# Strassen's products for q, k and v, attention per sequence of 64 keys, and the last sum of each rotation on GpSimd

## The reference, cut to what matters

```python
c = x @ W1.T + b1 + 2 * lora(x, adapter of the sequence)     # 1024 -> 1024
q = rope(c @ wq)   # 1024 -> 32 heads of 128
k = rope(c @ wk)   # 1024 ->  8 heads of 128
v = c @ wv         # 1024 ->  8 heads of 128
x1 = x + softmax(mask(q k^T / sqrt(128))) v @ wo             # 4096 -> 1024; the mask is causal within 64 tokens
out = x1 + ffn(cond2(x1))                                    # two more 1024 -> 1024 layers with routed low-rank parts
```

## Time and profile before

| what | value |
|---|---|
| runs, us | 2927.39, 2928.24, 2931.74; median 2928.24 |
| span of the profiled execution | 2929.6 us |
| TensorE busy | 2887.8 us, 99% |
| VectorE busy | 1516.9 us, 52% |
| ScalarE busy | 710.9 us, 24% |
| GpSimd busy | 478.3 us, 16% |
| mean granted TensorE clock | 0.996 |

### The profile page before, as it was taken

One profiled execution on the slowest core, in us unless ns is written; L12 is line 12 of the kernel. 1 busy time (PEld: TensorE's weight loads), 2 busy tenths in 40 slices (PEclk: granted clock), 3 DMA queues, 4 the chain that ended last, 5 costly groups with the idle time before them and its releaser, 6 DMA issues.

```text
span 2929.6 us, 39491 instructions
## 1 busy us (share of the span) xinstructions
PE 2887.8 (99%) x14200; PEld 2407.0 (82%) x14200; DVE 1516.9 (52%) x2443; ACT 710.9 (24%) x1681; POOL 478.3 (16%) x198
## 2 busy tenths in 40 slices
PE   8989999999999999999998999999999999999999
PEld 7867888888888888887876788888888888888887
DVE  2131656465665646565523265646556474656452
ACT  2121223132221313231102131313223131323110
POOL 0020111211111111110302012111111211111030
PEclk9999999999999999999999999999999999999999
DMA  6841111111111111111442111111111111110232
GB/s 214 233 121 37 43 44 36 43 43 42 37 43 43 36 43 43 37 35 55 111 144 60 43 37 49 37 43 36 43 43 36 44 39 45 37 43 29 72 99 68
DMA packets 230725, 174.67 MB, mean 60 GB/s; under 512 B 65146, under 2 KB 198394, under 8 KB 230658
## 3 DMA queue, kind: packets, MB, share of 16 engines
q1 hardware_dynamic: 202850, 151.80, 18.1%
q10 hardware_dynamic: 27808, 22.02, 2.3%
HBM read 151.58 MB, written 22.22 MB: 59 GB/s over the span
## 4 chain that ended last, share of the span: by engine, by line
PE 89%; DVE 5%; issue 2%; ACT 2%; SPq 1%; DMA 0%; ACTq 0%; DVEq 0%
PE prod L529 26%; PE prod L531 25%; PE prod L530 25%; PE turned L726 4%; PE turned L705 2%; PE turned L715 2%; ACT probs L1051 2%; DVE rope_sin L1372 2%; PE turned L523 1%; PE prod L625 1%; PE prod L888 1%; DVE row_max L1385 1%; DVE probs L1382 1%; PE turned L695 0%; PE prod L865 0%
## 5 line engine op out<-in xcount | busy, mean ns | idle before, releaser
L529 PE MATMUL prod<-c_hi,w_hi 128*128 128x512 f32 (+1 forms) x1856 | 737.7, 397 | 3.2 <-DVE c_lo L1445 3.2
L531 PE MATMUL prod<-c_hi,w_lo 128*128 128x512 f32 (+1 forms) x1856 | 724.3, 390 | 0.0
L530 PE MATMUL prod<-c_lo,w_hi 128*128 128x512 f32 (+1 forms) x1856 | 722.7, 389 | 0.0
L1193 POOL TENSOR_TENSOR w_lo<-raw,w_hi 128x1024 fp32r<-128x1024 f32 x160 | 382.1, 2388 | 1844.1 <-ACT w_hi L983 1844.1
L1434 DVE TENSOR_TENSOR x<-prod,x 128x512 f32<-128x512 f32 x512 | 349.4, 690 | 284.0 <-PE prod L531 281.4
L531 PEld LDWEIGHTS prod<-c_hi,w_lo 128*128 128x128 f32 (+1 forms) x1856 | 347.3, 187 | 75.9
L529 PEld LDWEIGHTS prod<-c_hi,w_hi 128*128 128x128 f32 (+1 forms) x1856 | 347.8, 187 | 74.1 <-DVE c_lo L1445 4.0
L530 PEld LDWEIGHTS prod<-c_lo,w_hi 128*128 128x128 f32 (+1 forms) x1856 | 348.1, 188 | 70.5 <-issue 1.0
L529 PE MATMUL prod<-o_hi,w_hi 128*128 128x512 f32 x1024 | 405.0, 395 | 0.0
L531 PE MATMUL prod<-o_hi,w_lo 128*128 128x512 f32 x1024 | 399.4, 390 | 0.0
L530 PE MATMUL prod<-o_lo,w_hi 128*128 128x512 f32 x1024 | 398.8, 389 | 0.0
(11 more groups left out here) (123 smaller groups left out, 2689.4 us busy)
## 6 DMA issues: line engine op xcount, KB each, us to landing
raw<-in_wq SPq DMA_DIRECT2D x64, 512.0 KB, 4.0
raw<-in_wo SPq DMA_DIRECT2D x64, 512.0 KB, 3.8
raw<-t_scratch SPq DMA_DIRECT2D x34, 512.0 KB, 3.5
t_scratch<-x ACTq DMA_DIRECT2D x17, 512.0 KB, 5.0
x_raw<-in_x SPq DMA_DIRECT2D x16, 512.0 KB, 8.8
raw<-in_wk SPq DMA_DIRECT2D x16, 512.0 KB, 3.6
raw<-in_wv SPq DMA_DIRECT2D x16, 512.0 KB, 3.6
raw<-m_scratch SPq DMA_DIRECT2D x16, 512.0 KB, 3.5
```

What stands on the lines that cost most here:

```text
L529: pe.matmul(dst, wh, xh, start=start, stop=False)
L530: pe.matmul(dst, wh, xl, start=False, stop=False)
L531: return pe.matmul(dst, wl, xh, start=False, stop=stop)
L1193: pool.tensor_tensor(WL[j % 2][:], RAW[j % 2][:], WH[j % 2][:].bitcast(F32), ALU.subtract).then_inc(split_d, 1)
```

## The change

**Products.** q, k and v no longer come from `main`. The output of two heads by two token blocks (a quad: k with v, q heads 0 and 1, q heads 2 and 3; three quads for each group) is a 2 x 2 block product with the 1024 inputs cut in two, done as seven products of 12 matmuls each. The seven right sides (`b11`, `b21`, `b22` and four sums) are made once for a half in the W1 stage, in high and low parts. The seven left sides of a quad are blocks or sums of blocks of the weights. GpSimd makes four sums and seven low parts of 512 columns for each quad (the list below), ScalarE the seven high parts (`s_high`). A quad's weights (1 MB) come in one buffer, `RAWP`. `SH`/`SL` have one buffer for each of the seven, so the next quad's high part i waits for product i of this one. ScalarE copies the first product out (`p1_copy`), and VectorE makes the outputs with seven additions of 512 columns; those of a head are added in place in PSUM and rotated from there. In the code PR_1 is product 0, then PR_2, PR_6, PR_7, PR_5, PR_4, PR_3.

**Rotation.** VectorE writes the cosine part to K or Q, and the sine part to a single `RS`; the sum of the two is now a GpSimd instruction (`rotated_sum`), placed between its weight work for the next quad. The next rotation waits for it.

**Attention.** A unit is two heads by 512 tokens, four units for each group. Scores are 16 matmuls of 64 x 64 outputs (`score`), the softmax works on eight blocks of 64 keys, with eight exponentials of 64 columns for each unit, the transposes are four for each unit (`turn_p`), and `pv` is eight matmuls over 64 keys (half the partitions) by 128 columns. v is transposed twice, once shifted by 64 tokens (`turn_v`, 16 transposes for each group). These pieces stand behind products of the next quads (the list `at_`); the last group's stand between the first wo products. The output goes to scratch DRAM by `o_out`: two ScalarE copies to one buffer and a store of 512 KB, each waiting for the store before.

**wo and W1.** The wo products leave the groups and follow all eight: 4 blocks of 1024 rows by 8 tiles by 2 token blocks, `main` each, the same count of matmuls. Their inputs are loaded from scratch (`load_o`, eight loads of 512 KB), and split in 16 pieces by ScalarE (`o_high`) and GpSimd (`o_low`). The W1 stage loads each weight tile twice, once for each token block (`T_WO` is 16 tiles), with the low parts on GpSimd. x goes back to scratch DRAM block by block (`x_back` on GpSimd, `store_xt`) and is read again as `X1`. x comes through four buffers: blocks 4 to 7 are loaded behind the 16 adapter loads in the first half. The second half's blocks 0 to 3 are transposed in the last blocks of the first half, and its 16 adapter loads stand before the load of the last weight tile there. All loops are unrolled in the program. The matmul columns of the first part and of the last stage are the same.

The diff, cut to the waits and orders that the text speaks of:

```diff
+            def store_xt(hf, b):
+                sp.wait_ge(x_sum, hf * TB + b + 1)
...
+            def load_w1(hf, n):
+                if n >= 2:
+                    sp.wait_ge(w_lo, pool_no(hf, n - 2) + 1)
+                load_tile(hf, n, t_d[TW_W + W1_ORDER[n][0]])
...
+            def load_pair(n, hf, g, qd):
+                if g == 0 and qd == 0:
+                    sp.wait_ge(w_lo, pool_no(hf, T_WO - 1) + 1)
+                else:
+                    sp.wait_ge(s_lo, 7 * (n - 1) + 6)
...
+            def load_o(hf, kb):
+                sp.wait_ge(o_stored, 16 * 4 * (hf * NKV + 2 * kb + 2))
+                if kb == 0:
+                    sp.wait_ge(qprod, q_done(pair_no(hf, NKV - 1, QD_23), 3))
...
+                for c in range(KC):
+                    sp.dma_start(chunk_of(o_lows(kb % 2, OWP), c), o_d[kb * KC + c]).then_inc(o_in[c], 16)
...
+                load_b1(hf, 0)
+                for n in range(2, T_WO):
+                    if n - 2 < TB:
+                        store_xt(hf, n - 2)
+                    load_w1(hf, n)
+                    if n == 10:
+                        sp.wait_ge(prod, q_base + QN["c7.0"] + 1)
+                        load_b1(hf, 1)
+                for g in range(NKV):
+                    for qd in range(QUADS):
+                        load_pair(pair_no(hf, g, qd), hf, g, qd)
+                load_wo(hf, 0)
...
-                    for j in range(12):
-                        main(Q_G + j, (j // TT) % 2, j % TT, CH, CL).then_inc(prod, 1)
+                def product(n, i, first):
+                    name, bank = BLOCKS[i], (7 * n + i) % 4
+                    gg, qd = divmod(n, QUADS)
+                    pg, pq = divmod(n - 1, QUADS)
+                    pe.wait_ge(s_lo, 7 * n + LOS[i])
+                    if i == 0 and first:
+                        pe.wait_ge(taken, q_base + Q_WO + 4)
+                    elif i == 0:
+                        pe.wait_ge(quad_in, quad_at(n - 1, A_U3))
+                    elif i in (1, 2) and not first and pq == QD_KV:
+                        pe.wait_ge(quad_in, quad_at(n - 1, (A_C22, A_C21)[i - 1]))
+                    elif i in (1, 2, 3) and not first:
+                        pe.wait_ge(rs_in, rotated_at(pg, pq, 1 if pq == QD_KV else i))
+                    elif i == 4:
+                        pe.wait_ge(p1_in, n + 1)
+                    elif i == 5:
+                        pe.wait_ge(rs_in, rotated_at(gg, qd, 0))
+                    elif i == 6:
+                        pe.wait_ge(quad_in, quad_at(n, A_U2))
                     hold(pe)
...
+                    for b in range(BPT):
+                        for r in range(2):
+                            for s in range(2):
+                                c = b * P + s * SEQ
+                                mm = pe.matmul(SCB[s * SEQ:(s + 1) * SEQ, b * P + r * SEQ:b * P + (r + 1) * SEQ],
+                                               Q[r][t][:, c:c + SEQ], K[:, t * NT + c:t * NT + c + SEQ],
+                                               start=True, stop=True)
...
+                    for b in range(2):
+                        for s in range(2):
+                            for r in range(2):
+                                rows = slice(r * SEQ, (r + 1) * SEQ)
+                                c = (2 * hb + b) * P + s * SEQ
+                                vv = v_block(2 * (t * BPT + 2 * hb + b) + s, r)
+                                o = b * P + s * SEQ
+                                mm = pe.matmul(view(OB[r], 2)[:, :, o:o + SEQ], VV[rows, vv:vv + HD],
+                                               view(PT[t][rows, :], 2)[:, :, c:c + SEQ], start=True, stop=True)
...
+                            at_ = (qd, i)
+                            if g:
+                                if at_ == (QD_KV, 0):
+                                    turn_p(gg - 1, 0, 1)
+                                if at_ == (QD_KV, 1):
+                                    score(gg - 1, 1, 0)
+                                if at_ == (QD_KV, 3):
+                                    score(gg - 1, 1, 1)
+                                if at_ == (QD_KV, 5):
+                                    turn_p(gg - 1, 1, 0)
+                                if at_ == (QD_KV, 6):
+                                    pv(gg - 1, 0, 0)
+                                if at_ == (QD_01, 0):
+                                    pv(gg - 1, 0, 1)
+                                    turn_p(gg - 1, 1, 1)
+                                if at_ == (QD_01, 1):
+                                    pv(gg - 1, 1, 0)
+                                if at_ == (QD_01, 2):
+                                    pv(gg - 1, 1, 1)
+                            if at_ == (QD_01, 2):
+                                turn_v(gg, 0)
+                            if at_ == (QD_01, 3):
+                                turn_v(gg, 1)
+                            if at_ == (QD_01, 4):
+                                turn_v(gg, 2)
+                            if at_ == (QD_01, 5):
+                                turn_v(gg, 3)
+                            if at_ == (QD_23, 1):
+                                score(gg, 0, 0)
+                            if at_ == (QD_23, 3):
+                                score(gg, 0, 1)
+                            if at_ == (QD_23, 5):
+                                turn_p(gg, 0, 0)
...
+                def o_out(gg, t, hb):
+                    w = 4 * gg + 2 * t + hb
+                    act.wait_ge(pv_done, w + 1)
+                    if w:
+                        act.wait_ge(o_stored, 16 * w)
+                    for r in range(2):
+                        ins = act.copy(OS_[:].rearrange("p (q r n) -> p r q n", q=2, r=2)[:, r], view(OB[r], 2))
+                    ins.then_inc(o_taken, 1)
...
+                        p1_copy(n)
+                        if qd == QD_KV and g:
+                            p_out(4 * (gg - 1) + 1)
+                        if qd == QD_01 and g:
+                            p_out(4 * (gg - 1) + 3)
+                            o_out(gg - 1, 0, 1)
+                        if more:
+                            s_high(n + 1, 0)
+                            s_high(n + 1, 1)
+                        if qd == QD_01 and g:
+                            o_out(gg - 1, 1, 0)
+                        if more:
+                            s_high(n + 1, 2)
+                        if qd == QD_KV and g:
+                            exps(4 * (gg - 1) + 2)
+                        if qd == QD_23:
+                            exps(4 * gg)
+                        if qd == QD_01:
+                            if g:
+                                o_out(gg - 1, 1, 1)
+                            v_out(gg, 0)
+                            v_out(gg, 1)
+                        if more:
+                            s_high(n + 1, 4)
+                            s_high(n + 1, 3)
+                        if qd == QD_KV and g:
+                            exps(4 * (gg - 1) + 3)
+                        if qd == QD_23:
+                            exps(4 * gg + 1)
+                        if qd == QD_01:
+                            v_out(gg, 2)
+                        if more:
+                            s_high(n + 1, 5)
+                        if qd == QD_01:
+                            v_out(gg, 3)
+                        if qd == QD_KV and g:
+                            p_out(4 * (gg - 1) + 2)
+                        if qd == QD_23:
+                            p_out(4 * gg)
+                        if more:
+                            s_high(n + 1, 6)
+                        if qd == QD_KV and g:
+                            o_out(gg - 1, 0, 0)
+                last = pair_no(hf, NKV - 1, QD_23)
+                last_gg = hf * NKV + NKV - 1
...
+                x_back(0)
+                for n in range(2, T_WO):
+                    tile_lo(hf, n)
+                    if 1 <= n - 1 < TB:
+                        x_back(n - 1)
...
+                def rotated_sum(n, i):
+                    pool.wait_ge(rs_in, rotated_at(gg, qd, i))
+                    pool.tensor_tensor(dst, dst, RS[:], ALU.add).then_inc(rotated, 1)
...
+                    pool.wait_ge(pair_in, 32 * (n + 1))
+                    pool.tensor_tensor(ta, a21, a22, ALU.add).then_inc(s_sum, 1)
+                    pool.wait_ge(s_sum, 4 * n + 1)
+                    pool.tensor_tensor(tb, ta, a11, ALU.subtract).then_inc(s_sum, 1)
+                    low(0, a11, 1)
+                    low(1, a12, 2)
+                    pool.wait_ge(s_sum, 4 * n + 2)
+                    low(2, tb, 3)
+                    if n > n0:
+                        rotated_sum(n - 1, 0)
+                    pool.wait_ge(s_lo, 7 * n + 3)
+                    pool.tensor_tensor(tb, a12, tb, ALU.subtract).then_inc(s_sum, 1)
+                    low(4, ta, 4)
+                    pool.wait_ge(s_lo, 7 * n + 4)
```

(66 more changed lines are left out.)

1514 lines of the change are left out of this document (841 added, 673 removed).

## The result

The changed kernel takes **3049.28 us** (median of 4 runs, 3046.80 to 3053.11) where the kernel before took 2929.31 beside it (2927.39 to 2931.74): ratio 1.0411, 95% interval 1.0397 to 1.0426. So it is 120 us slower. The forecast was 3095, with a range of 2930 to 3190 and slower at 0.82: the sign is right, the size 46 us too high.

What follows compares the result with a forecast made beforehand. The prediction took TensorE, busy 99% of the span, as the bound. Its terms, -131 + 21 + 147 + 15 + 42 + 73 = +167 us, gave 3097 on the profiled time, 3095 us on the median; range 2930 to 3190.

Steps and rivals of the forecast that it cites:

- The products: Quads' matmuls: 252 a group instead of 288, over 16 groups at 0.2267 us each, -131 us.
- the start of the first quad: Into each half's first quad: ScalarE's casts wait for VectorE's chain of seven sums, 7.6 us a half, +15.
- W1's chain of 11.5 us: W1 stage: x_back, DMA start, load, cast and low part in sequence for tiles 3 to 8; whole W1 term +73 us.
- The sum of the quads' waits: Inside the quads: fixed engine orders make TensorE wait 10.1 us in 14 groups, 2.3 in each half's first, +147.
- the forecast's three: Inside the quads: transposes of probs wait for normalise at 0.7, 1.3 and 0.7 us, each with 0.5 added.
- The forecast's wait of pv on its copy: Quad kv, behind product 6: pv waits 1.8 us for a copy standing late in ScalarE's order.
- Attention on TensorE: Each group's scores, transposes, pv and changes between kinds: 21.0 us against 19.7 before, +21 us in all.
- halves of the array work side by side: Score and pv matmuls: neighbours on different halves run at double rate, -86 us, giving 3010; chance 0.13.
- the rival's 36: Attention on TensorE: each change of tiling mode drains the engine, +36 us, giving 3131; chance 0.05.
- wo start: Into wo: TensorE waits for GpSimd's last rotation and low parts, 21 us a half, +42.
- GpSimd the slower kind: Quads, wo and W1: GpSimd takes 1.75 us for 512 columns instead of 1.33, giving 3177; chance 0.08.
- TensorE hardly waits in the quads: Inside the quads: waits stay under 1.2 us a group, -147 us, giving 2948; chance 0.18.

Runs made afterwards that it cites:

- Experiments 2 to 4: Separate edits of the changed kernel: W1 load ahead of store, 2995.75 us; three normalise steps earlier on VectorE, 2991.86; ScalarE's v_out(2) ahead of cast 3, 3021.94.
- experiment 7: The changed kernel with neg_max, the scaled negative maximum, moved from VectorE to ScalarE: 3046.97 us, ratio 1.0399.
- experiment 3: The changed kernel with three normalise steps moved up in VectorE's order: 2991.86 us, ratio 1.0211.
- experiment 8: The changed kernel with all orders mended: 2875.96 us; rotated sum also back on VectorE: 2865.73; x blocks 4 to 7 also handled ahead of adapters: 2857.71.

## Why the prediction was right, and where it was off

- **What held.** The products at -131, the start of the first quad (15, measured 16) and W1's chain of 11.5 us (11.6) came out as worked out. So did the kind of wait inside the quads and their sum (147, measured 144). Experiments 2 to 4 take most of these waits away by the order that the forecast blamed, so these causes are shown, not only their sizes.
- **The sum of the quads' waits is partly luck.** `turn_p` on normalise was larger, 77.4 us where the forecast's three come to 59: these waits are 1.7 to 2.1 each but for two, not 0.7 to 1.3 (1.2 to 1.8 with the 0.5 added), which I put down to `neg_max` and `normalise` waiting for GpSimd up to 1.1 us each (experiment 7). The first group of each half was larger too (7.3 at `turn_v`, where 2.3 was allowed). Smaller was `v_out(0)`, mostly 0.5 to 0.7 us or none instead of 2.5, since the stores land in 2.9 us and not 4 to 5. The forecast's wait of pv on its copy did not show (experiment 3); in its place pv waited 18.1 us on `o_out`, which the forecast had not named.
- **The step that failed** is "Attention on TensorE", in the price of a score pass ("I take 0.07, the nearest") and a pv pass (0.111): they cost 0.034 and 0.068, and the term, by these prices, was about -86 instead of +21. The cause is the rival "halves of the array work side by side", to which I gave 0.13. I had a row against it, the load side busy 82%, but that row is of the long matmuls, and says nothing of neighbours on different halves (a score's load lasts 0.138 us here, one of a long matmul 0.19).
- **A term was missing, and it hid more than half of this.** The forecast let waits cost their idle time and nothing else, and said of the clock only that under W1's chain "a slower matmul mostly hides". Outside W1 slower long matmuls cost some 37 us and the 0.16 behind each wait's start some 19. So the time came within 46 us of 3095 because about -107 and +56 stood against each other, with +12 in W1 and -8 in the smaller terms. The rival's 3010, 39 below the measured time, is missed for the same reason.
- **Its own signs of being wrong.** The forecast named three. Two came true, score and pv in pairs and stores that land in 3 us; the third, W1 loads that overlap `x_back`, did not. The direction held all the same, since the waits and W1 (144, 16, 36 and 85) outweigh the 131 and the 33.
- The Trainium skill (TensorEngine Tiling (Array Packing), Key Properties) says that different tiles load and multiply in parallel. The trace agrees: 0.034 a pass with halves in turns, 0.057 with the same half again. By the same page a change of mode drains TensorE. The trace leaves room for a small cost: a score set begins 0.33 us behind the long matmul ahead of it (431.13 to 431.46), where in the kernel before a set that uses the whole array begins 0.23 behind (469.81 to the 470.04 of the earlier trace rows). On the way back both cost the same, the second long matmul standing 0.33 and 0.31 behind the first:

```profile
469.81 0.39 PE L531 MATMUL prod<-c_hi,w_lo 128*128 128x512 f32 x1
...
472.18 0.48 PE L529 MATMUL prod<-c_hi,w_hi 128*128 128x512 f32 x1
472.49 0.40 PE L530 MATMUL prod<-c_lo,w_hi 128*128 128x512 f32 x1
```

  At 0.09 to 0.10 for each of the 128 sets this is some 12 us, a third of the rival's 36; no run separates the change of mode from other reasons.
- **W1** is 12 us larger than forecast, 50 for 45 in the first half and 35 for 28 in the second. In the first, tile 2 is ready at 203.1 (forecast 203), the low-rank matmul of tile 8 starts at 288.9 (by the forecast's sum 286.5), and the seven tiles behind it take 47.6 us for 44.5, at a granted clock of 0.95. For the second half the runs leave the cause open.
- **wo start** is 6 smaller than forecast.
- **GpSimd the slower kind** (0.08): its 512 columns took 1.27 to 1.33, the forecast's 1.33. Out.
- **TensorE hardly waits in the quads** (0.18), the other side: false for the orders as written. With the orders mended the waits inside the quads still come to some 64 us (26.4, 23.7 and 14.4 in the table of experiment 8), some 4 a group against the 1.2 that this rival asked for. What I called "a fixed order, not a load" was right, and it is also the reason that more than half of it could be undone.

## What to carry to other kernels

A saving on the bound engine can be lost as long as the others' orders are not written for the new pace: here 131 us of matmuls were saved and 252 us of idle time came in, and small changes of order, with one sum moved back, took 192 us off again. Where four engines run fixed lists, look at each wait's instruction and ask what stands ahead of it on its own engine and whether that could stand behind it; then look again, since half of what you take away may turn up one step later. And price a small matmul by its neighbours, not only by its shape: two score passes on different halves of the array took 0.068 us here, two on the same half 0.114. A wait costs more than its idle time: look at the distances of the matmuls behind it too.

## What the hardware showed that I had not expected

- Matmuls on different halves of the array, issued in turns: 0.034 us for 64 columns and 0.068 for 128 in float32, those of the score and pv sets; 0.057 and 0.101 when neighbours share a half (in pv also a PSUM bank).
- A VectorE instruction of 8 columns took up to 1.285 us (median 1.255, shortest 0.171) in the changed kernel; the one at 416.13 ended with GpSimd's instruction. The Trainium skill (SBUF — State Buffer, Who interferes with whom) describes the ports of the two as a lock held for a whole instruction, and the second to come as blocked; the trace agrees at 416.13 and 424.80, and experiment 7 adds that sparing one such instruction hands about half of the wait to the next.
- The 2.1 us wait of TensorE at 426.57 was followed by six long matmuls about 0.43 apart instead of 0.23, 1.2 us more on top of the wait. Of the 14 waits of 2.1 us at this place of a group, 8 were followed by such matmuls, at once or within 1.5 us, and 6 by none (594.7 for one); so such a wait does not always bring them. The 28 waits of 1.7 us at L852 were followed by none.
